# Attention scores as sixteen 32-row fp32 products instead of four 128-row products with a block-diagonal key matrix

## The reference

```python
# attention: 16 heads of 32, 128 keys
q = (layernorm(x) @ Wq.T + bq)      # 2 x 2048 x 512, split in 16 heads
k = (ctx @ Wk.T + bk); v = (ctx @ Wv.T + bv)
att = einsum('bhsd,bhtd->bhst', q, k) / sqrt(32)     # the scores
att = where(mask == 0, -1e9, att)
x = x + tanh(g_xattn) * einsum('bhst,bhtd->bhsd', softmax(att), v)
# feed-forward: a shared expert, and 2 of 8 experts per token
x = x + tanh(g_ffn) * (routed_experts(layernorm(x)) + shared_expert(layernorm(x)))
```

## Time and profile before

| | |
|---|---|
| runs of the kernel before | 1147.19, 1142.1 and 1141.54 us, median 1142.1 |
| the profiled execution | 1144.73 us, of which the span of instructions is 1143.0 us |
| TensorE busy | 1046.4 us, 92% of the span |
| VectorE, ScalarE, GpSimd busy | 788.8, 498.1, 444.1 us |
| granted TensorE clock, mean | 0.952 |

### The profile page before, as it was taken

One profiled execution on the slowest core, in us unless ns is written; L12 is line 12 of the kernel. 1 busy time (PEld: TensorE's weight loads), 2 busy tenths in 40 slices (PEclk: granted clock), 3 DMA queues, 4 the chain that ended last, 5 costly groups with the idle time before them and its releaser, 6 DMA issues.

```text
span 1143.0 us, 30439 instructions
## 1 busy us (share of the span) xinstructions
PE 1046.4 (92%) x9392; PEld 761.0 (67%) x9393; DVE 788.8 (69%) x2813; ACT 498.1 (44%) x1010; POOL 444.1 (39%) x654
## 2 busy tenths in 40 slices
PE   5898989999999999870799999999999999999997
PEld 4587768777877877760355555555555888888885
DVE  5899778888888888774576666666665445455455
ACT  2465546666666666641354444444443111111111
POOL 4344546666666666543221122112110322232322
PEclk9998889999999999965899999999999999999999
DMA  7463563334433323430433333433342555545554
GB/s 267 184 237 137 161 175 96 94 94 94 94 94 94 94 94 94 112 89 24 134 116 113 116 110 119 120 110 117 114 127 68 165 160 162 174 158 170 151 173 138
DMA packets 76735, 147.02 MB, mean 129 GB/s; under 512 B 20912, under 2 KB 23088, under 8 KB 73872
## 3 DMA queue, kind: packets, MB, share of 16 engines
q1 hardware_dynamic: 46512, 66.01, 19.5%
q0 software_dynamic: 12896, 35.58, 11.5%
q10 hardware_dynamic: 17280, 44.83, 10.6%
HBM read 94.04 MB, written 52.35 MB: 128 GB/s over the span
## 4 chain that ended last, share of the span: by engine, by line
PE 61%; issue 11%; DVE 11%; POOL 8%; ACT 3%; DMA 3%; POOLq 1%; another core or an unknown queue 1%; SPq 0%; DVEq 0%; ACTq 0%
PE bank L1046 8%; PE bank L1048 8%; PE bank L1047 8%; PE bank L1038 7%; PE bank L1240 5%; PE bank L1241 5%; PE bank L1242 5%; PE bank L1091 4%; DVE arena L779 3%; PE bank L1111 3%; POOL arena L468 3%; PE bank L1251 2%; PE bank L1252 2%; PE bank L1253 2%; POOL token_of_row L504 2%
## 5 line engine op out<-in xcount | busy, mean ns | idle before, releaser
L1038 PE MATMUL bank<-ident,arena 128*128 128x128 f32 (+1 forms) x1336 | 169.4, 275 | 49.9 <-DMA arena<-normed_rows,arena 25.6
L1038 PEld LDWEIGHTS bank<-ident,arena 128*128 128x128 f32 (+1 forms) x1336 | 144.7, 139 | 88.7 <-issue 67.4
L1241 PE MATMUL bank<-arena,weights 128*128 128x128 f16 x1024 | 174.9, 218 | 0.1
L1240 PE MATMUL bank<-arena,weights 128*128 128x128 f16 x1024 | 174.9, 220 | 0.0
L1242 PE MATMUL bank<-arena,weights 128*128 128x128 f16 x1024 | 174.8, 218 | 0.0
L515 POOL DMA_INDIRECT arena<-normed_rows,arena x71 | 67.1, 946 | 251.8 <-PE bank L1038 234.6
L1046 PE MATMUL bank<-weights,arena 128*128 x426 | 162.0, 380 | 2.1 <-ACT arena L648 1.9
L1047 PE MATMUL bank<-weights,arena 128*128 x426 | 161.8, 380 | 0.0
L1048 PE MATMUL bank<-weights,arena 128*128 x426 | 161.8, 380 | 0.0
L1111 PEld LDWEIGHTS bank<-arena 128*128 128x128 f32 x1024 | 131.9, 199 | 38.0 <-issue 31.9
L1091 PE MATMUL bank<-arena 128*128 128x512 f32 x256 | 145.7, 675 | 7.7 <-DVE arena L779 7.0
(11 more groups left out here) (180 smaller groups left out, 2207.1 us busy)
## 6 DMA issues: line engine op xcount, KB each, us to landing
expert_rows<-arena ACTq DMA_DIRECT2D x71, 256.0 KB, 2.1
arena<-in_x SPq DMA_DIRECT2D x64, 256.0 KB
weights<-in_w_gu ACTq DMA_DIRECT2D x8, 1024.0 KB, 4.9
x_rows<-arena SPq DMA_DIRECT2D x32, 256.0 KB
normed_rows<-arena SPq DMA_DIRECT2D x32, 256.0 KB
normed_transposed<-arena SPq DMA_DIRECT2D x32, 256.0 KB
arena<-normed_transposed SPq DMA_DIRECT2D x32, 256.0 KB
arena<-x_rows SPq DMA_DIRECT2D x32, 256.0 KB
```

The costliest lines, as they stand in the source:

```text
L1038: last = t.transpose(dst[:, c * P:(c + 1) * P], src[:, c * P:(c + 1) * P], (ident16 if src.dtype == F16 else ident)[:, :])
L1240: t.matmul(dst, shared(c, part, 0, dc), x_hi_c, start=(c == 0), stop=False)
L1241: t.matmul(dst, shared(c, part, 0, dc), x_lo_c, start=False, stop=False)
```

## The change

The block-diagonal matrix goes. `k_t` holds the keys as they come out of the projection, 128 rows by 128 keys for each chunk and batch. The weights' columns are reordered on the host so that chunk c holds head 4 g + c on its rows 32 g to 32 g + 31 (row group g). A head's scores are then one fp32 product of 32 rows by 128 columns. `scores(k)` is called for k = 0 and 2, and makes eight products: for each chunk one of row group k into bank 2 and one of row group k + 1 into bank 3. It waits for the maxima of both former contents of the banks. On VectorE `maxima(1)` follows `maxima(0)` directly and the small work stands behind both. TensorE's order becomes scores(0), mix_values(0), mix_values(1), turn_probs(2), scores(2), turn_probs(3). The memset of `kbd` and its 16 evictions of 32 rows become 4 evictions of 128 rows. The bytes set aside in the arena are unchanged.

```diff
--- before.py
+++ after.py
@@ -141,7 +141,8 @@
             return arena[:, top[0] - cols:top[0]]
 
         wq = carve(EC * E).bitcast(F16).rearrange("p (a n) -> p a n", a=2)
-        kbd = carve(B * EC * HG * T).rearrange("p (b c n) -> p b c n", b=B, c=EC)
+        k_t = carve(B * EC * T).rearrange("p (c b t) -> p c b t", b=B, c=EC)
+        carve((HG - 1) * B * EC * T)
         vaug = carve(B * H * (D + 1)).rearrange("p (b h d) -> p b h d", b=B, h=H)
         score = [carve(H * T) for _ in range(2)]
         wk_s = score[0].rearrange("p (c n) -> p c n", c=EC)
@@ -202,7 +203,7 @@
         PASS2_END = top[0]
 
 
-        SCORES_END = EC * E + B * EC * HG * T + B * H * (D + 1) + 2 * H * T
+        SCORES_END = EC * E + HG * B * EC * T + B * H * (D + 1) + 2 * H * T
         PLAN = NX * NT + 3 * NX + NX * NX + 2 * SLOTS * NX + 2 * SLOTS + NT * TOP * NX
         top[0] = SCORES_END - PLAN
         assert top[0] >= PASS2_END
@@ -701,7 +702,6 @@
         def _(dve):
             d = nc.vector
 
-            d.memset(kbd, 0.0).then_inc(kv_set, 1)
             dve.wait_ge(pool_set, 6)
             d.memset(vaug[:, :, :, D:D + 1], 1.0)
             dve.wait_ge(wq_in, 16)
@@ -751,13 +751,10 @@
 
             def keys_and_values():
                 dve.wait_ge(small_in, 96)
-                dve.wait_ge(kv_set, 1)
+                dve.wait_ge(kv_mm, 1)
                 for c in range(EC):
-                    dve.wait_ge(kv_mm, 1)
-                    for h in range(HG):
-                        rows = slice(h * D, (h + 1) * D)
-                        last = d.tensor_scalar(kbd[rows, :, c, h * T:(h + 1) * T], bank[K_BANK + c][rows, 0:B * T].rearrange("p (b t) -> p b t", b=B),
-                                               bk_s[rows, c:c + 1], float(D) ** -0.5, ALU.add, ALU.mult)
+                    last = d.tensor_scalar(k_t[:, c], bank[K_BANK + c][:, 0:B * T].rearrange("p (b t) -> p b t", b=B),
+                                           bk_s[:, c:c + 1], float(D) ** -0.5, ALU.add, ALU.mult)
                 last.then_inc(kv_set, 1)
                 dve.wait_ge(kv_mm, 2)
                 for b in range(B):
@@ -808,6 +805,7 @@
                     dve.wait_ge(hi_ready, n + 1)
                     d.scalar_tensor_tensor(x_lo, bank[0][:, :], X_SCALE, x_hi, ALU.mult, ALU.subtract).then_inc(lo_ready, 1)
                 maxima(0)
+                maxima(1)
                 if live(n8, NT):
                     dve.wait_ge(rank_done, n8 + 1)
                     if live(n7, NT):
@@ -819,7 +817,6 @@
                     d.tensor_reduce(logit_top, bank[1][:, 0:NX], AX.X, ALU.max, negate=True).then_inc(logit_max, 1)
                     dve.wait_ge(logit_max, n7 + 1)
                     d.tensor_scalar(logit_neg, logit_top, w_back[:, 4:5], None, ALU.mult).then_inc(logit_shift, 1)
-                maxima(1)
                 normalise(1, 5)
                 if live(n5, NT):
                     dve.wait_ge(res_here[u5], 16 * (j5 + 1))
@@ -1085,11 +1082,16 @@
                     n, j, u = tile(J, v, 3)
                     if live(n, NT):
                         pe.wait_ge(q_ready, n + 1)
-                        need(pe, max_done, group(n, k - 2))
+                        need(pe, max_done, group(n, k - 1))
                         if it_is_first(n, k):
-                            pe.wait_ge(kv_set, 2)
-                        t.matmul(bank[2 + k % 2][:, :], q_t[u][:, k * P:(k + 1) * P], kbd[:, u, k, :],
-                                 start=True, stop=True).then_inc(s_done, 1)
+                            pe.wait_ge(kv_set, 1)
+                        for c in range(EC):
+                            for g in (k, k + 1):
+                                rows = slice(g * D, (g + 1) * D)
+                                mm = t.matmul(bank[2 + g % 2][:, c * T:(c + 1) * T], q_t[u][rows, c * P:(c + 1) * P],
+                                              k_t[rows, c, u, :], start=True, stop=True)
+                                if c == EC - 1:
+                                    mm.then_inc(s_done, 1)
 
                 def turn_probs(k):
                     n, j, u = tile(J, v, 4)
@@ -1104,7 +1106,7 @@
                         pe.wait_ge(pt_ready, group(n, k))
                         half = k // 2
                         if it_is_first(n, k):
-                            pe.wait_ge(kv_set, 3)
+                            pe.wait_ge(kv_set, 2)
                         need(pe, attn_done[half], n)
                         for h in range(HG):
                             at = (k % 2 * HG + h) * (D + 1)
@@ -1132,12 +1134,10 @@
                 turn_probs(0)
                 turn_probs(1)
                 scores(0)
-                scores(1)
                 mix_values(0)
+                mix_values(1)
+                turn_probs(2)
                 scores(2)
-                mix_values(1)
-                scores(3)
-                turn_probs(2)
                 turn_probs(3)
                 n, j, u = tile(J, v, 6)
                 if live(n, NT):
@@ -1282,6 +1282,10 @@
         w = w.reshape(*w.shape[:-2], w.shape[-2] // P, P, w.shape[-1])
         return np.ascontiguousarray(np.moveaxis(w, -2, 0))
 
+    def by_row_group(w):
+
+        return np.moveaxis(w.reshape(*w.shape[:-1], HG, H // HG, D), -3, -2).reshape(w.shape)
+
     def cols(b):
         return np.ascontiguousarray(b.reshape(EC, P).T)
 
@@ -1293,11 +1297,11 @@
         "pad": np.broadcast_to(got["mask_Bx1x1xS2_ik0"].reshape(1, B, T), (P, B, T)),
         "sub": got["mask_1x1xSxS2_ik0"],
         "gates": np.broadcast_to(np.concatenate([got["g_xattn"], got["g_ffn"]]).reshape(1, 2), (P, 2)),
-        "wq_t": rows(got["L0_xattn_Wq"].T),
-        "wk_t": rows(got["L0_xattn_Wk"].T),
+        "wq_t": rows(by_row_group(got["L0_xattn_Wq"].T)),
+        "wk_t": rows(by_row_group(got["L0_xattn_Wk"].T)),
         "wv_t": rows(got["L0_xattn_Wv"].T),
-        "bq": cols(got["L0_xattn_bq"]),
-        "bk": cols(got["L0_xattn_bk"]),
+        "bq": cols(by_row_group(got["L0_xattn_bq"])),
+        "bk": cols(by_row_group(got["L0_xattn_bk"])),
         "bv": np.broadcast_to(got["L0_xattn_bv"].reshape(1, E), (P, E)),
         "router": rows(got["L0_ffn_router"]),
         "w_gu": rows(gate_up),
```

## The result

The kernel with 32-row products takes 1173.12 us in the median of four runs (1157.02 to 1187.38), the kernel before 1142.55 (1141.54 to 1147.19). The ratio of the comparable runs is 1.0172, 95% interval [1.0123, 1.0222]: slower, by 1.2 to 2.2%. A second set of runs on another chip gave 1.0199 [1.0139, 1.0258].

A forecast was written before the change was run, and what follows sets the result against it. The prediction took a ring of VectorE, GpSimd and ScalarE, 27.74 us a turn, as the bound. Its terms summed to -2.3 us, 1144.73 to 1142.4 for the profiled execution, which stood 2.6 above the median: 1140 us, range 1132 to 1164.

The forecast's parts named there:

- one-stream rival: Score pairs on TensorE: row groups alternate without overlap, a pair readable after 2.34 us; 1162 us, chance 0.22.
- its own sign of being wrong: First pass: pairs overlap and the pass still changes by more than 6 us; then TensorE or its clock was a link.
- the one it followed: Pass 1's loop: one 27.74 us turn, its ring VectorE 9.9, GpSimd 10.2, ScalarE 7.6 us, TensorE no link.
- A pair of products: Eight small score products on TensorE: two row groups run side by side, 0.90 us a pair against 1.71.
- the 0.13 us in hand: Even iteration, VectorE's first reading of scores: 0.13 us to spare before the score product is late.
- Fill of the array when the row groups change: TensorE, at changes of row group: +0.5 us in the sum.
- Loads hidden, order, small work moved: Pass 1: loads run under streaming, the new order loses nothing, moved VectorE work saves 1.5 us and 0.5 us.
- Keys: Key evictions: sixteen become four, 5.9 us less, but 0.4 saved and 5.5 become VectorE's wait before L764.
- Long spells at half clock: First pass: three spells of halved TensorE clock, each about 1.1 us shorter; -3.2 us.
- What TensorE's free time does: Odd iteration, before the second layernorm's transposes: 1.9 us idle may halve the clock, in half of ten turns; +2.3 us.
- the clock falls more often: First pass: pairs overlap, but more TensorE idle halves the clock in every turn; +13 us, 1153 us, chance 0.08.
- load not hidden: Score pairs on TensorE: each product's load adds to its stream, a pair readable after 3.9 us; 1227 us, chance 0.11.

The follow-up runs named there:

- rows64: The `order_only` kernel with score products of 64 rows by 256 columns, two row groups taking turns; ratio 1.0132 to the kernel before.
- order_only: The kernel before with only the changed kernel's order, keeping 128-row by 512-column products and block-diagonal keys; ratio 0.9972.
- rows32_wide_b: The kernel before with each score product using only the first 32 rows of its operands, still 512 columns; ratio 1.0721.
- mode_changes_b: The kernel before with a 32-row product of 8 columns ahead of each score product, eight row-tiling changes a tile; ratio 0.9991.
- rows32_old_order: The changed kernel's 32-row products in the order of the kernel before, all four of a row group together; ratio 1.0607 to the kernel before.
- split128: The kernel before with each 512-column score product cut into four of 128 columns, still 128 rows; ratio 1.0030.
- after_dense32_b: The changed kernel with three dense 32-row products before the values and three before scores(2); ratio 1.0410 to the kernel before.
- after_dense_inside: The changed kernel with three dense 128-row by 512-column products behind scores(0) and three before scores(2); ratio 1.0327 to the kernel before.
- after_fill: The changed kernel with four dense 128-row by 512-column products, results overwritten, at the head of each iteration with scores; ratio 1.0204 to the kernel before.
- before_fill: The kernel before with four dense 128-row by 512-column products, results overwritten, at the head of each iteration with scores; ratio 0.9898.
- order_fill: The `order_only` kernel with four dense 128-row by 512-column products, results overwritten, at the head of each iteration; ratio 0.9890 to the kernel before.

## Why the prediction was wrong

Predicted were 1140 us within 1132 to 1164, with 0.33 for no change; measured are 1173 us and a ratio of 1.0172. That the comparable runs, at some 1162 us, fall inside the range is luck: its upper end came from the one-stream rival, which did not happen. The prediction gave its own sign of being wrong, overlapping pairs and a pass that changes by more than 6 us; both came, and with them what it concluded from it, that TensorE's clock was a link in more turns than the one it followed. By its own steps:

- *A pair of products*: side by side was taken, 0.90 us, and 1.09 measured. The row groups do overlap, 1.69 / 1.09 = 1.55 times; the estimate of 1.2 us from the Trainium skill (TensorE: Matmul & The Clock Gate, Part 3) was nearer. Of the rule told beside it from the Trainium skill (TensorE: Matmul & The Clock Gate, Part 3), that a load runs under another product only if its row group differs, the prediction says that the trace is silent; its own figures speak against it, since the transposes load 128 columns (0.101 us) and stream 128 (0.107) in 0.112 us, all on the same rows. The 0.2 us are a mis-sized term, and more than the 0.13 us in hand: at full clock the first reading waits 0.90 us at 404.26. The kernel after has no turn without half clock (the least has 10.2 us), but `rows64` has, with pairs of 1.06 us, and they take 27.6 us like those of `order_only`, whose pairs take 1.72: nothing of the time comes from this term there.
- *Fill of the array when the row groups change*, +0.5: no row stood behind it. The runs show longer work on TensorE with changes of row tiling (1.91 us for 1.71 in `rows32_wide_b`) and, in `mode_changes_b`, no loss of time by it.
- *Loads hidden, order, small work moved*: right. The order alone is 0.9972, where 2.0 us less were forecast for it and none can be told from the interval; its turns at full clock are 27.6 us, as forecast.
- *Keys*: right. The eviction became one group of 1.64 us, and a wait of 4.9 us (5.5 forecast) came ahead of L761. That it starts at 32.84 us, 1.9 earlier where 0.4 was forecast, is for the most part because the product it waits for began 1.5 us earlier in this execution.
- *Long spells at half clock*: wrong in sign. They were priced at three, each 1.1 us shorter. They became longer, a mean of 11.6 us against 4.8: at half clock nothing in the tile ends them before the queries (15 of 17).
- *What TensorE's free time does*, +2.3 us, with its rival "the clock falls more often", +13 us at a chance of 0.08: together with the term above, -3.2, this is the step that failed, the price of the half clock. The two add up to -0.9 us, and the turns give +42. That time at half clock would be added was right, and both the mechanism and the size were wrong. The step took idle time for the only thing that lowers the clock, since every spell of before has idle time ahead of it, and so looked for 1.9 us of idle before the second layernorm's transposes. That idle hardly exists in the kernel after: TensorE waits there 3.6 us in the whole pass, in 4 waits. Where it does come, in `rows64` (9.5 us in 9 waits, up to 1.4), no spell begins right behind it. The 128-row score products were what ended the spells of before, and the change took them out. In the kernel after the spells still start behind short idle times (all 17 have some in the 7.5 us before), but with 32 rows they last. No term of the sum had a price for what a product does to the clock.
- *One stream, load not hidden*: both false by 1.09 us a pair. The forecast's mark for the one stream, a wait of VectorE of 35 us or more, came true with 59.7 us and would have misled: it is mostly the halved clock, and only the length of a pair tells the two apart.

That products of 32 rows are the cause is shown by three pairs that differ in little else: `rows32_wide_b` against before (180 and 58 us of half clock, 1.0721 and 1), `rows32_old_order` against `split128` (188 and 48; 1.0607 and 1.0030), `after_dense32_b` against `after_dense_inside` (179 and 105; 1.0410 and 1.0327). The mean clock over whole executions says the same in each pair: 0.881 and 0.954, 0.885 and 0.950, 0.894 and 0.923. `rows64` lies between (0.927). Order, stream length and changes of row tiling are each ruled out by a run of their own. Not told apart are the rows at work at one time and the rows of one product: `rows64` has all 128 at work in two products, and still has twice the half-clock time of `order_only` (81 and 41 us); its shorter pairs also leave more idle time (TensorE is busy 398 of the 460 us, against 418). That the lower clock is what costs the time rests on the turns: 0.30 us for each us of half clock, which gives 42 us for the 42.6 between the spans (with the luck said above). By the ratio, the kernel after loses less than `rows32_old_order`, though with the same half-clock time; the overlapped pair is 0.6 us shorter, at full clock, than the serial one, which no run prices alone.

Open: why four 32-row products at the head serve the kernel before nearly as well as 128-row ones, when 32-row products inside the tile don't serve the kernel after. What surrounds them differs (128-row scores right behind them, or small ones), and no run changed that alone. Open too is why `after_fill` loses in the iterations ahead of the loop what it gains in it; that its four products take 1.02 us at full clock, so up to 2 us at half, and outlast an idle time like the 1.35 us they stand in, is an argument and not shown.

## What to carry to other kernels

Don't price a smaller product by its length at full clock alone. A product with fewer rows may do the same work in less time and still lose, if it takes away the full-array streams that kept the clock up or brought it back: read the granted clock around the product that you replace, and ask what ends the half-clock stretches there. Where TensorE is idle before such a stretch, a few products without a use are cheap, and may pay: `before_fill` and `order_fill` beat the kernel before by 1.0% and 1.1%, while `after_fill` gained nothing.

## What the hardware showed that was not expected

- TensorE's clock fell to its lower level in the middle of unbroken work: 21 of 28 falls in `rows32_old_order` and 24 of 29 in `rows32_wide_b` had under 0.05 us of idle in the 7.5 us before them. The Trainium skill (TensorE: Matmul & The Clock Gate, Part 1) ties the clock to how busy TensorE has been; these rows show it busy by the profile and slow, so busy time as the profile counts it is not what decides.
- Products of 512 fp32 columns hold the clock with 128 rows and not with 32 (58 and 180 us of half clock; `before` and `rows32_wide_b`).
- Two row groups overlap by 1.55 times with fp32 products of 128 columns (0.106 us a record for one, 0.068 for two in turns). Eight changes of row tiling a tile, with four small products, lengthen TensorE's work by about 1.0 us a tile, and cost nothing that a ratio of 0.9991 [0.9967, 1.0015] could show where TensorE isn't waited for.
